# Where VectorE takes the statistics of the first output half: between the two additions, or behind the second one

## The reference, cut to what matters

```python
x = L0_attn_x                                             # (4, 2048, 512)
x = _layernorm(x + _rwkv6_tmix(x, ...), axis=-1)
x = _layernorm(x + _ffn(x, ...), axis=-1)

def _layernorm(x, axis=-1, eps=1e-05):
    m = jnp.mean(x, axis=axis, keepdims=True)
    v = jnp.var(x, axis=axis, keepdims=True)
    return (x - m) / jnp.sqrt(v + eps)

# inside the mixer: the last step, and the decay that each tile's state needs
w = time_decay + jnp.tanh(xw @ td_w1) @ td_w2
decay = jnp.exp(-jnp.exp(w))
...
return y * g @ Wo.T                                       # Wo: 512 x 512
```

## Time and profile before

| | |
|---|---|
| median of 3 runs | 2955.86 us (2953.89 to 2955.86) |
| the profiled execution: its own time | 2956.85 us |
| its span in the trace | 2955.0 us |
| TensorE busy | 2871.2 us, 97% of the span |
| VectorE busy | 2469.3 us, 84% |
| ScalarE busy | 1991.6 us, 67% |
| GpSimd busy | 949.4 us, 32% |
| a tile of the loop, mean of 29 | 89.32 us |

### The profile page before, as it was taken

One profiled execution on the slowest core, in us unless ns is written; L12 is line 12 of the kernel. 1 busy time (PEld: TensorE's weight loads), 2 busy tenths in 40 slices (PEclk: granted clock), 3 DMA queues, 4 the chain that ended last, 5 costly groups with the idle time before them and its releaser, 6 DMA issues.

```text
span 2955.0 us, 101539 instructions
## 1 busy us (share of the span) xinstructions
PE 2871.2 (97%) x40221; PEld 2115.4 (72%) x40221; DVE 2469.3 (84%) x5308; ACT 1991.6 (67%) x4242; POOL 949.4 (32%) x788
## 2 busy tenths in 40 slices
PE   6799999999999999999999999999999999999997
PEld 4577776777776777777777777777777777777775
DVE  7788888888888888889888889888889888888887
ACT  5476666776666776666776667766667766667764
POOL 4222333323333323333323332223333233333232
PEclk8899999999999999999999999999999999999998
DMA  5000000000000000000000000000000000000000
GB/s 218 9 17 20 20 24 16 21 20 16 23 24 13 24 20 16 23 24 13 20 24 16 23 22 15 20 23 16 23 16 21 20 16 23 24 13 24 20 16 23
DMA packets 22055, 72.42 MB, mean 25 GB/s; under 512 B 2816, under 2 KB 3072, under 8 KB 20000
## 3 DMA queue, kind: packets, MB, share of 16 engines
q1 hardware_dynamic: 21664, 66.12, 6.6%
HBM read 49.33 MB, written 16.78 MB: 22 GB/s over the span
## 4 chain that ended last, share of the span: by engine, by line
PE 91%; DVE 4%; issue 1%; ACT 1%; DVEq 0%; POOL 0%; POOLq 0%; ACTq 0%
PE psP L454 22%; PE psF L704 16%; PE psF L717 15%; PE psP L680 7%; PE psP L498 7%; PE psW L537 4%; PE psY L580 2%; PE psY L596 2%; PE psW L520 2%; PE psX L399 2%; DVE ARENA L1265 1%; PE psP L476 1%; PE psX L432 1%; PE psX L568 1%; PE psW L559 1%
## 5 line engine op out<-in xcount | busy, mean ns | idle before, releaser
L454 PE MATMUL psP<-ARENA,WALL 128*128 128x256 f32 x3072 | 694.7, 381 | 2.7 <-ACT ARENA L844 2.7
L779 ACT ACTIVATE ARENA<-ARENA 32x512 f32<-32x512 f32 (+3 forms) x930 | 524.3, 564 | 165.6 <-DVE ARENA L1343 69.5
L454 PEld LDWEIGHTS psP<-ARENA,WALL 128*128 128x128 f32 x3072 | 575.3, 191 | 79.6 <-issue 3.5
L1542 DVE SCALAR_TENSOR_TENSOR HIDDEN<-GG,FWB,HIDDEN 128x128 f16<-128x128 f32 x1024 | 347.6, 399 | 295.2 <-ACT HIDDEN L990 294.0
L1024 POOL TENSOR_TENSOR MT<-ARENA 32x256 fp32r<-32x256 f32 x330 | 349.1, 1058 | 422.8 <-ACT ARENA L779 394.2
L704 PE MATMUL psF<-XHI,WFC 128*128 128x128 f16 x4032 | 480.8, 220 | 1.6 <-DVE ST L1565 1.6
L704 PE MATMUL psF<-XLO,WFC 128*128 128x128 f16 x4032 | 479.3, 220 | 0.0
L717 PE MATMUL psF<-WPJ,HIDDEN 128*128 128x512 f16 x2016 | 473.2, 380 | 2.0 <-ACT GG L981 2.0
L1037 POOL TENSOR_TENSOR ARENA<-ARENA,XT 128x1024 f32<-128x1024 f32 x128 | 279.5, 2184 | 493.4 <-DVE ARENA L1265 478.7
L704 PEld LDWEIGHTS psF<-XHI,WFC 128*128 128x128 f16 x4032 | 391.7, 98 | 40.2 <-issue 32.5
L704 PEld LDWEIGHTS psF<-XLO,WFC 128*128 128x128 f16 x4032 | 395.7, 98 | 17.6 <-issue 10.3
(11 more groups left out here) (199 smaller groups left out, 5015.5 us busy)
## 6 DMA issues: line engine op xcount, KB each, us to landing
XT<-x_ch SPq DMA_DIRECT2D x33, 520.0 KB, 4.3
ARENA<-x_tok SPq DMA_DIRECT2D x32, 512.0 KB, 3.9
out<-OUTX SPq DMA_DIRECT2D x64, 256.0 KB, 2.0
WALL<-w_all SPq DMA_DIRECT2D x5, 1024.0 KB, 19.2
ARENA<-wfc SPq DMA_DIRECT2D x3, 1024.0 KB, 11.2
WPJ<-wfc SPq DMA_DIRECT2D x1, 1024.0 KB, 17.2
WPJ<-wpj SPq DMA_DIRECT2D x1, 1024.0 KB, 21.3
GG<-wpj SPq DMA_DIRECT2D x1, 1024.0 KB, 23.3
```

Of the source, the lines that this page charges most:

```text
L454: mm = pe.matmul(psP[:, P.bank(f"{name}{g}"), COLS * c:COLS * (c + 1)], WALL[:, w, k, 128 * (2 * g + c):128 * (2 * g + c + 1)], cc(XF[slot ...
L779: return act.activation(o, i, ACT.Copy)
L1542: e = dve.scalar_tensor_tensor(out=HLO[:, k, :], in0=GG[:, u % 2, 0, 128 * m:128 * (m + 1)], scalar=FWB[:, 0, k:k + 1], in1=HHI[:, k, :], ...
```

## The change

`bn_stats` of both halves moves out of the loop over the halves into a second loop behind it. The addition of the second half then follows directly on the mixing terms `mk`, and the two `bn_stats` follow on that. Nothing else is changed, neither the waits nor the other engines.

```diff
                 for p in range(PAIRS):
                     dve.wait_ge(p_full, P.full(it, f"wo{p}"))
                     dve.tensor_tensor(X1[:, p, :], psP[:, P.bank(f"wo{p}"), :], XTOK[:, p, :], ALU.add).then_inc(p_dve, 1)
                     if p == 0:
                         decay_input(it)
                         dve.wait_ge(tm_ready, M.read(it, "w1b"))
                         mix(it + 1, 1, "mk", None)
+                for p in range(PAIRS):
                     dve.wait_ge(p_dve, P.read(it, f"wo{p}"))
                     dve.bn_stats(BNS[:, p, :], X1[:, p, :]).then_inc(bn_done, 1)
                 dve.wait_ge(bn_done, 2 * it + 2)
```

## The result

The changed kernel takes 2937.54 us (median of 4 runs, 2934.93 to 2938.76) against 2955.16 us for the kernel before (4 runs, 2953.89 to 2955.86): a ratio of 0.994, 95% interval 0.9922 to 0.9957, or 17.6 us. Measured a second time, in 5 runs beside other kernels, the ratio was 0.9946 (0.9932 to 0.9959). The forecast was 2938.7 us and 17.2 us.

What follows compares the result with a forecast made beforehand. TensorE, busy 97% of the span, was taken as the bound, waiting 0.69 us per tile for VectorE's second addition. 30 x 0.55 + 0.60 + 0.10 = 17.2 us gave a median of 2938.7 us; range 2936 to 2946.2 us.

Steps and rivals of the forecast that it cites:

- The addition starts 0.60 us earlier, and all of it arrives at L476: VectorE's second-half addition takes bn_stats' slot; TensorE's td2 load gains the whole 0.60 us, about 0.09 us of waiting stays.
- The keys now wait for GpSimd, 0.12 us behind its addition, and about 0.05 us is lost: At L454, TensorE's keys wait for GpSimd's L1037; the load is 0.15 us late, head start absorbing most.
- 0.55 us per seam: Gain each time td2 (L476) waits for the second addition: 0.60 - 0.05 us, 30 times; bounds 0.30 and 0.60 us.
- The 0.11 us of the second `bn_stats` gets lost in L1503: On VectorE behind the addition, 0.11 us saved gains nothing in the loop, as GpSimd's addition holds tiny L1503.
- VectorE still waits 0.20 us at its next meeting: At L1565, VectorE's wait for TensorE falls from 0.75 to 0.20 us, so VectorE is not late.
- The first seam gives 0.60 us once: Between tile 0 and tile 1, the keys' load waits for ScalarE, so the full 0.60 us counts once.
- 0.10 us behind the last tile: Behind the last tile, where GpSimd has no addition, the earlier second bn_stats gains 0.1 us.
- The time of the whole: Whole kernel: 17.2 us less, median 2938.7 us, which is 0.58% less.
- The slower rival: VectorE's moved addition holds up GpSimd's last MT piece, delaying the keys: 5.9 us more, 2961.8 us; chance 0.04.

Runs made afterwards that it cites:

- extra_ahead: Kernel before, with one more bn_stats of the first half, into an unread buffer, in front of the second addition; 2975.98 us, ratio to before 1.0074.
- sums_late: Changed kernel with the last addition of the feed-forward's sums moved from ahead of the first addition to behind the small L1504; 2937.15 us, ratio 0.9943.
- pool_before: Kernel before, with one small power operation on GpSimd in front of its addition to the keys; 2955.15 us, ratio 1.0001.
- pool_after: Changed kernel, with one small power operation on GpSimd in front of its addition to the keys; 2951.66 us, ratio to before 0.9988.
- changed_again: The changed kernel run once more, with nothing altered; 2939.83 us, ratio to before 0.9946.
- extra_behind: Changed kernel, with one more bn_stats of the first half behind the second addition; 2936.93 us, ratio to before 0.9944.
- mk_behind: Changed kernel, with the second addition moved further up, ahead of the mixing terms mk; 2946.88 us, ratio to before 0.9974.
- quarter_first: sums_late, with the first 2 of the late product's 8 matmuls done ahead of L476 instead of behind it; 2938.36 us, ratio to before 0.9943.

## Why the prediction was right, point by point

- *The addition starts 0.60 us earlier, and all of it arrives at L476.* Right: L476's wait among the loads fell from 0.89 to 0.30 us. extra_ahead shows the same slope on the other side: 0.59 us more of waiting for 0.60 us of work.
- *The keys now wait for GpSimd, 0.12 us behind its addition, and about 0.05 us is lost.* Right, and shown: against L476 the first load of L454 came 0.15 us later than before, the second 0.04 us (medians over the loop), and 70 us into the tile the stream was 0.06 us later. sums_late, where the keys do not wait for GpSimd, gets these 0.06 us back. pool_before and pool_after show that the room of before is used up.
- *0.55 us per seam.* The tiles without the pause give 0.53 us, and 0.54 us by changed_again. The mean distances give 0.57 us (89.32 - 88.76) and 0.48 us by changed_again; they differ by how many tiles of an execution have the pause.
- *The 0.11 us of the second `bn_stats` gets lost in L1503.* Right: the `bn_stats` now take 1.27 us together, and L1504 grew from 1.09 to 1.22 us. It ends with GpSimd's addition in the kernel before, the changed one, extra_behind, pool_before and pool_after, whatever its length (0.62 to 1.63 us).
- *VectorE still waits 0.20 us at its next meeting.* Measured 0.20 us.
- *The first seam gives 0.60 us once.* Right, by the weight loads at the place itself: from the last load of `wo1` (L680) to the first of L476 it was 6.30 us before and is 5.70 us now, and the keys follow L476 by 2.53 us in both. The first two rows are those of the kernel before:

```profile
127.61 0.19 PEld L680 LDWEIGHTS psP<-WALL,ARENA 128*128 128x128 f32 x1 [0.24 <-issue]
133.91 1.00 PEld L476 LDWEIGHTS psP<-TZ,TD 64*128 64x128 f32 x16 [0.91 <-issue]
...
125.98 0.19 PEld L680 LDWEIGHTS psP<-WALL,ARENA 128*128 128x128 f32 x1 [0.24 <-issue]
131.68 1.00 PEld L476 LDWEIGHTS psP<-TZ,TD 64*128 64x128 f32 x16 [0.32 <-issue]
```

- *0.10 us behind the last tile.* Right: from the last load of L680 to the load of L711, which waits for VectorE there, it was 6.95 us and is 6.83 us.
- *The time of the whole.* The terms as measured make 30 x 0.53 + 0.60 + 0.12 = 16.6 us, the medians of the runs differ by 17.6 us, and the forecast was 17.2 us. That the last two agree within 0.4 us is partly luck. The load of L476 in tile 2 comes at 221.2 to 225.4 us in the twelve profiles, the stretch behind the load in tile 31 takes 137.5 to 140.3 us, and the pause adds some 0.2 us in a changing number of tiles; the runs of the changed kernel spread over 3.8 us.
- *The slower rival*, that the addition holds up the last piece of `MT`, did not happen: the pair still took 1.52 us.

## What to carry to other kernels

When one engine is the bound and another releases it once per tile, look at the last few instructions ahead of that release: what the released engine does not need can go behind it, and counts one to one. Then follow the released engine to its next wait, and subtract the time from the release there to its start; if the room is about as large as the gain, that other engine is the next limit. Stop at the point where the work ahead of the release is work that the waiting engine itself feeds; moving the addition beyond it only moved the wait here (mk_behind). And when such a change is worth a few hundredths of a microsecond per tile, compare tile by tile: here the mean and the time of the whole hid in sums_late and quarter_first what the undisturbed tiles show.

## What the runs showed of the hardware

- A VectorE instruction of 128x2 elements took 0.17 us alone and up to 1.63 us beside a GpSimd addition, and ended 0.02 us behind that addition (pool_after; 0.03 us in the kernel before). 0.60 us of other VectorE work in front of it cost nothing (extra_behind).
- From the end of a GpSimd addition to the weight load that waits for it through a register instruction passed 0.12 us, and the profile files the gap under "issue".
- A late first load does not delay its matmul stream in full: 0.15 us late at the load was 0.04 us at the second load, and 0.06 us at 70 us into the tile.
- A stream of matmuls can stand still for 0.15 to 0.53 us without a recorded wait, at one fixed place of its list, in some passes of the loop and not in others (4 of 29 and 16 of 29 in two executions of one kernel). Its cause is open.
